# The first pair of rows of the first cross attention, made inside the last two heads of the first self attention

## The reference

```python
x = x + _L0_attn_ref(_layernorm(x), Wq, Wk, Wv, Wo, quadrant_weights)   # 16 heads of 16, 1024 x 1024 scores each
x = x + _L0_xattn_ref(_layernorm(x), ctx, ctx, ..., mask)               # below
x = x + _L0_ffn_ref(_layernorm(x), ...)                                 # top 2 of 8 experts, capacity 320
x = x + _L1_attn_ref(...); x = x + _L1_xattn_ref(...); x = x + _L1_ffn_ref(...)

def _L0_attn_ref(...):
    attn = softmax((q1 @ k_eff1.T + q2 @ k_eff2.T) * scale)
    return (attn @ v) @ Wo

def _L0_xattn_ref(q, k, v, ...):        # q: normalised x, k = v: the context
    qh, kh, vh = heads(q @ Wq.T + bq), heads(k @ Wk.T + bk), heads(v @ Wv.T + bv)
    scores = where(mask, qh @ kh.T / sqrt(16), -1000)
    return (softmax(scores) @ vh) @ Wo.T + bo
```

## Time and profile before

| | us |
|---|---|
| median of 3 runs | 1724.78 (1718.09 to 1725.84) |
| the profiled execution | 1716.94 |
| its span, first to last instruction | 1715.1 |
| mean granted TensorE clock, share of full speed | 0.969 |
| plain scores of the self attention (L2210), first to last start | 65.4 to 444.4 |
| turned scores of the self attention (L2219), first to last start | 84.4 to 465.2 |

### The profile page before, as it was taken

The page is one execution under the profiler, slowest core; times in us unless marked ns, Lnnn a source line. Parts: engine busy times, 40 slices in busy tenths (PEclk is TensorE's granted clock), DMA queues, the critical chain, the costliest instruction groups (busy, mean ns, idle before and its releaser), DMA issues. The chain is left out here.

```text
span 1715.1 us, 31331 instructions
## 1 busy us (share of the span) xinstructions
PE 1563.5 (91%) x10661; PEld 1106.5 (65%) x10662; DVE 973.9 (57%) x1748; ACT 585.2 (34%) x1167; POOL 404.9 (24%) x544
## 2 busy tenths in 40 slices
PE   6999999999889825999999999999989949999996
PEld 5733434343367624777777777856657649999995
DVE  7688888888369876221111211378879863444443
ACT  3277777777635500111111111034346500000000
POOL 1000000000022202233312211156652103333331
PEclk9999999999999966999999999999999969999998
DMA  2112221111401111133322331200015126666674
GB/s 75 39 46 66 58 55 47 42 45 43 166 21 36 45 51 32 22 99 104 102 64 52 95 89 16 55 11 1 2 59 175 50 90 175 176 179 181 181 183 117
DMA packets 89077, 134.90 MB, mean 79 GB/s; under 512 B 17568, under 2 KB 66080, under 8 KB 88832
## 3 DMA queue, kind: packets, MB, share of 16 engines
q1 hardware_dynamic: 73824, 113.05, 20.9%
q0 software_dynamic: 15168, 20.72, 7.6%
HBM read 98.00 MB, written 20.84 MB: 69 GB/s over the span
## 5 line engine op out<-in xcount | busy, mean ns | idle before, releaser
L2117 DVE TENSOR_REDUCE mx<-ps 128x1 f32<-128x1024 f32 x256 | 300.2, 1215 | 59.1 <-PE ps L2210 59.1
L1286 PE MATMUL ps<-xTe,wide 128*128 128x320 f32 x1024 | 277.2, 432 | 0.1
L1286 PEld LDWEIGHTS ps<-xTe,wide 128*128 128x128 f32 x1024 | 194.4, 190 | 80.2 <-issue 0.3
L1355 DVE TENSOR_TENSOR hTe<-prT,ps 128x320 f32<-128x320 f32 x128 | 62.4, 488 | 214.3 <-ACT prT L1327 214.1
L2016 ACT ACTIVATE wide<-ps 128x512 f32<-128x512 f32 x256 | 138.9, 599 | 61.0 <-PE ps L2219 61.0
L2016 ACT ACTIVATE turns_of_use<-ps 128x512 f32<-128x512 f32 x256 | 139.2, 600 | 59.1 <-PE ps L2219 58.8
L2219 PE MATMUL ps<-QS,KS 99*128 99x512 bf16 x512 | 154.2, 381 | 2.0 <-ACT wide L2016 0.8
L1445 PEld LDWEIGHTS ps<-xw_all,w1t 128*128 128x128 f32 x1248 | 145.3, 192 | 3.6 <-issue 0.9
L1445 PE MATMUL ps<-xw_all,w1t 128*128 128x128 f32 x1248 | 145.8, 275 | 1.2 <-ACT xw_all L1477 1.2
L1327 ACT ACTIVATE prT<-ps 128x320 f32<-128x320 f32 x128 | 55.9, 437 | 262.3 <-PE ps L1286 262.3
L1462 PE MATMUL ps<-wide,hTm 128*128 x624 | 141.0, 379 | 0.0
(11 more groups left out here) (305 smaller groups left out, 2328.9 us busy)
## 6 DMA issues: line engine op xcount, KB each, us to landing
w1t<-in_L_ffn_w SPq DMA_DIRECT2D x39, 1024.0 KB
wide<-in_L_ffn_gate_weight SPq DMA_DIRECT2D x8, 1024.0 KB, 5.5
wide<-_L_ffn_ff_pre_act_weight SPq DMA_DIRECT2D x8, 1024.0 KB, 8.6
wide<-L_ffn_ff_post_act_weight SPq DMA_DIRECT2D x8, 1024.0 KB, 10.9
wide<-in_L_ffn_w SPq DMA_DIRECT2D x1, 8192.0 KB, 27.2
QS<-wide SPq DMA_DIRECT2D x192, 32.0 KB, 2.0
KS<-wide SPq DMA_DIRECT2D x192, 32.0 KB, 2.0
VS<-V_all SPq DMA_DIRECT2D x32, 128.0 KB, 2.1
```

The source lines that it names most:

```text
L1286: ins = pe.matmul(ps[:, 3 + 2 * (q % 2) + n, 0:HC], wt[:, k, f * P:f * P + P], xTe[:, k, hf * HC:hf * HC + HC], start=(k == 0), stop=(k == ...
L1355: v.tensor_tensor(hTe[:, f, hf * HC:hf * HC + HC], sgt[:, q % 2, :], ps[:, 4 + 2 * (q % 2), 0:HC], ALU.mult).then_inc(f_m.sem, 1)
L2117: v.tensor_reduce(mx[:, s, t:t + 1], ps[:, 2 * (t % 2):2 * (t % 2) + 2, :], AX.XY, ALU.max).then_inc(h_rm.sem, 1)
```

## The change

Three parts.

1. Pair 0's rows, context, set-up, queries and first scores move from behind meeting 1 into heads 30 and 31. PE gets six blocks, each between two pieces of its attention work: turn pair 0's rows, the context, and the projection in head 30; turn the normalised rows, the queries and the scores in head 31. They use banks 0 (`FORE`) and 1 (`FORE_OWN`) in place of 7 and 6, and 2 and 3 as before. DVE gets `dve_first_rows` at the end of its part of head 30 and `dve_first_queries` at the end of its part of head 31, and does there what ACT did for this pair: the copies to `oT1` and `xT`, the normalised rows and the queries with their bias. POOL finishes pair 0's factors and adds the bias of pair 0 ahead of meeting 1.
2. The cross attention begins with pair 1's rows and pair 0's softmax. `keep_going(pe, 18, 1)` is gone. On DVE, pair 1's addition and statistics now stand between the two halves of pair 0's softmax; they stood before both.
3. `V_all` and `QS` are allocated first among the attention's tiles, so that the cross attention's tiles that are written early lie over `V_all`, whose last part has been read by then (`dve_first_rows` waits for the loads `h_ld` of all four slots).

```diff
+        V_all = sbA("V_all", [P, B, H, TB, 32])
+        QS = sbA("QS", [P, 4, S], BF16)
         turns_of_use = sbA("turns_of_use", [P, 4096])
...
+        def pe_first_rows(pe):
+            pe.wait_ge(x_ld, X_LOADS[0])
+            pe.wait_ge(h_rm.sem, h_rm.upto(B * H - 1))
+            pe_turn(pe, O_all[:, 0:2, :], x_ta, FORE)
+        def pe_first_projection(pe):
+            pe.wait_ge(x_oa.sem, x_oa.upto(0))
+            pe_out_rows(pe, oT1, woA, FORE_OWN, x_wa)
+        def pe_first_turn(pe):
+            pe.wait_ge(x_xn.sem, x_xn.upto(0))
+            pe_turn(pe, xn[:, 0, :, :], x_tb, FORE)
+        def pe_first_scores(pe):
+            pe.wait_ge(x_cr.sem, x_cr.upto(0))
+            pe.wait_ge(x_ra.sem, x_ra.upto(0))
+            pe_scores(pe, 0, 0, 0)
+        def dve_first_rows(v, c):
+            for sl in range(4):
+                v.wait_ge(h_ld[sl].sem, h_ld[sl].upto(B * H // 4 - 1))
+            v.wait_ge(x_ta.sem, x_ta.upto(0))
+            v.tensor_copy(oT1[:], by_chunk(FORE)).then_inc(x_oa.sem, 1)
+            dve_set_up(v, c, 0)
+            v.wait_ge(x_wa.sem, x_wa.upto(0))
+            v.tensor_tensor(pair_rows(0), pair_rows(0), ps[:, FORE_OWN, :].rearrange("p (j d) -> p j d", j=2), ALU.add)\
+                .then_inc(x_ra.sem, 1)
+            v.wait_ge(x_ra.sem, x_ra.upto(0))
+            c(row_stats(v, 0, 2))
+            begin_factors(v, 0, 2, x_fia)
+        def dve_first_queries(v):
+            v.wait_ge(x_fa.sem, x_fa.upto(0))
+            for t in range(2):
+                ins = v.tensor_scalar(xn[:, 0, t, :], xr[:, t, :], nv[:, 0, t:t + 1], nmr[:, t:t + 1], ALU.mult, ALU.add)
+            ins.then_inc(x_xn.sem, 1)
+            v.wait_ge(x_tb.sem, x_tb.upto(0))
+            v.tensor_copy(xT[:, 0, :, :], by_chunk(FORE)).then_inc(x_xt.sem, 1)
+            v.wait_ge(x_q.sem, x_q.upto(0))
+            for m in range(KC):
+                ins = v.tensor_scalar(qT[:, m, :], ps[:, FORE, m * 256:m * 256 + 256], float(DH) ** -0.5,
+                                      bq4[:, m:m + 1], ALU.mult, ALU.add)
+            ins.then_inc(x_qe.sem, 1)
...
             for i in range(-2, NP + 3):          # DVE
...
                 if here(i):
                     softmax(i, U, 0)
+                if layer == 0 and i == 0:
+                    v.wait_ge(x_wa.sem, x_wa.upto(1))
+                    add_rows(1, OWN, x_ra, 1)
+                    factors(1, x_fia)
...
-                if layer == 0 and here(i + 2):
+                if layer == 0 and 1 < i + 2 < NP:
...
-                if layer == 0 and i == -1:
-                    keep_going(pe, 18, 1)
...
             ahead_scores(t) of PE's head, called with t = 0, 2, 4, 6:
+                    elif (hh, t) == (2, 0):
+                        pe_first_rows(pe)
+                    elif (hh, t) == (2, 2):
+                        pe_context(pe, 0)
+                    elif (hh, t) == (2, 4):
+                        pe_first_projection(pe)
+                    elif (hh, t) == (3, 2):
+                        pe_first_turn(pe)
+                    elif (hh, t) == (3, 4):
+                        pe_queries(pe, 0, FORE)
+                    elif (hh, t) == (3, 6):
+                        pe_first_scores(pe)
```

More of the change, by code:

```diff
@@ L634, in act_cross @@
                     probs_turned(of(layer, i), 0)
-                if layer == 0 and here(i + 1):
+                if layer == 0 and 0 < i + 1 < NP:
                     queries(of(layer, i + 1))
@@ L785, in pool_cross, with pe_turn @@
                     end_factors(pool, c, i - 1, x_fid, x_fd, of(layer, i - 1))
-                if layer == 0 and here(i + 2):
-                    add_bias(i + 2, i + 2)
-        def pe_turn(pe, rows, done):
+                if layer == 0 and 0 < i + 2 < NP:
+                    pool_bias(pool, i + 2, i + 2)
+        def pe_turn(pe, rows, done, bank=TURN):
             for k in range(KC):
                 for j in range(2):
-                    ins = pe.transpose(ps[:, TURN, (2 * k + j) * P:(2 * k + j + 1) * P],
+                    ins = pe.transpose(ps[:, bank, (2 * k + j) * P:(2 * k + j + 1) * P],
@@ L794, in pe_turn, with pe_out_rows, pe_queries @@
                                        rows[:, j, k * P:(k + 1) * P], ident[:])
             ins.then_inc(done.sem, 1)
+        def pe_out_rows(pe, oT_, wo, bank, done):
+            for j in range(2):
+                for k in range(KC):
+                    ins = pe.matmul(ps[:, bank, j * 256:j * 256 + 256], oT_[:, k, j * P:j * P + P], wo[:, k, :],
+                                    start=(k == 0), stop=(k == KC - 1))
+            ins.then_inc(done.sem, 1)
+        def pe_queries(pe, U, bank):
+            pe.wait_ge(x_xt.sem, x_xt.upto(U))
+            for m in range(KC):
+                for k in range(KC):
+                    ins = pe.matmul(ps[:, bank, m * 256:m * 256 + 256], xw["q"][:, k, m * P:m * P + P],
+                                    xT[:, 0, k, :], start=(k == 0), stop=(k == KC - 1))
+            ins.then_inc(x_q.sem, 1)
@@ new lines, in pe_scores @@
+        def pe_scores(pe, u, U, j):
+            pe.wait_ge(x_qe.sem, x_qe.upto(U))
+            pe.wait_ge(x_sm.sem, x_sm.upto(U, j))
+            for m in range(KC):
+                for r in range(2):
+                    rows = slice(64 * r, 64 * r + 64)
+                    ins = pe.matmul(ps[:, r, m * 256:m * 256 + 256], qT[rows, m, j * P:j * P + P],
+                                    Kbd[rows, u // 4, m, :, :].rearrange("p h k -> p (h k)"),
+                                    start=True, stop=True)
+            ins.then_inc(x_s.sem, 1)
@@ L823, in pe_cross @@
         def pe_cross(pe, layer, left=None):
[L824 to L835, removed]
             def turn_prev(u):
@@ L843, in project_prev @@
                 pe.wait_ge(x_ra.sem, x_ra.upto(u - 1))
-                out_rows(oT1, woA, OWN, x_wa)
+                pe_out_rows(pe, oT1, woA, OWN, x_wa)
             def turn_out(u, U):
@@ L866, in logits @@
                 ins.then_inc(x_lg.sem, 1)
[L868 to L877, removed]
             def turn_probs(U, j):
@@ L908, in pe_cross @@
                 U = of(layer, i)
-                if i == -layer:
+                if layer == 1 and i == -1:
                     pe.wait_ge(x_cr.sem, x_cr.upto(layer))
-                if here(i):
-                    scores(i, U, 0)
+                if here(i) and (layer, i) != (0, 0):
+                    pe_scores(pe, i, U, 0)
                 if here(i - 1):
@@ L2144, in head @@
                     maxima(n + 2, hh % 2, 2, 8)
+                if last and hh == 2:
+                    dve_first_rows(v, c)
+                if last and hh == 3:
+                    dve_first_queries(v)
             maxima(0, 0, 0, 8)
```

55 lines of the change are left out of this document (25 added, 30 removed).

## The result

The changed kernel takes 1710.82 us (median of 6, 1708.83 to 1713.40) against 1724.42 (1718.09 to 1725.84): ratio 0.9933, 95% interval 0.9916 to 0.9951. It is faster by 13.6 us between the medians; by the ratio it is 0.7%, or 11.6 us (8.4 to 14.5). Forecast were 13.3 us and 1711.5.

A forecast was written before the change was run, and what follows sets the result against it. Around meeting 1 every engine waits for the next in a chain; in heads 30 and 31 PE and ACT take turns. The forecast was 1724.78 + 4.6 - 17.9 = 1711.5 us, range 1702 to 1719.5.

The forecast's parts named there:

- The meeting, +4.6: Heads 30 and 31: PE's 8.24 us of moved blocks, partly covered by waits, make meeting 1 4.6 us later.
- DVE under the blocks: Heads 30 and 31: DVE has 3.7 us to spare before head 30's division, so its new queue costs nothing.
- Behind the meeting, 12.8: From meeting 1 to pair 1's first scores: a chain of 12.8 us, before 30.69, so 17.9 us gone.
- No PE gap over 1.7 us: Behind meeting 1: the walk of the new order finds no PE gap longer than 1.7 us.
- a granted clock of 0.5 behind the meeting: Sign of being wrong: PE granted half clock behind meeting 1, where full clock was expected from 440 to 590.
- `keep_going` worth nothing: Kernel before, behind meeting 1: the 36 products, 4.18 us, ran during DVE's set-up and are worth nothing by themselves.
- The freely running watch: PE's clock: the same gap need not cost 1.7 us in another execution; gain then 11.6 instead of 13.3 us.
- Layout, later stages: The new allocation is priced at 0, up to 1 us either way; later stages start earlier and are the same.
- Sum: Whole kernel: +4.6 for the later meeting less 17.9 behind it gives -13.3 us.
- Uncovered blocks (9.2): Rival, 14%: in heads 30 and 31 PE's 8.24 us, with waits 9.2, come on top; gain 7.0 or 5.3 us.
- A longer chain through DVE (18): Rival, 8%: pair 1's scores no earlier than 18 us behind meeting 1; gain 8 us, time 1716.7.
- A clock that stays low: Rival, 4%: half clock at meeting 1 and the pairs behind; three pairs would give +26 us, 1751.

The follow-up runs named there:

- e4: The changed kernel with head 31's blocks (turn, queries, scores of pair 0, and their DVE and POOL work) put back behind meeting 1; trace span 1709.8 us.
- e5: The changed kernel with the context's 16 products made twice over in head 30; trace span 1713.5 us.
- e8: The changed kernel with five extra 128x1024 reductions on DVE in front of head 30's division; trace span 1716.2 us.
- e9: The changed kernel with products nobody reads filling PE's waits at the end of the first cross attention; ratio to the kernel before 0.9914.
- e3: The kernel before without the 18 `keep_going` products in turn -1; ratio to the kernel before 1.0014.
- e1: The kernel before with only the new layout, `V_all` and `QS` allocated first; ratio to the kernel before 1.0001.
- e11: The kernel before with products nobody reads filling the end of its first cross attention; ratio to the kernel before 0.9994.
- e0: The changed kernel once more, unedited; 1707.82 us against 1721.36 for the kernel before, ratio 0.9913.
- e6: The changed kernel with pair 1's addition and statistics on DVE behind both halves of pair 0's softmax; trace span 1716.0 us.
- e10: The changed kernel with products nobody reads at meeting 1 and at the end of the cross attention; ratio to the kernel before 0.9914.
- e12: The changed kernel with pair 1's addition behind both softmax halves and products nobody reads filling meeting 1; trace span 1718.0 us.

## Why the prediction was right

- **The meeting, +4.6.** Measured +5.0 (403.5, and 408.4 to 408.5 in two traces). Head 30: 3.0 forecast, 3.2 by e4; head 31: 1.6 forecast, 1.75. The misses are small: normalised rows 0.73 us on DVE, so PE's second turn waited 0.33 us. The step that each block's cover must be looked for piece by piece is confirmed by e5, where a block without cover costs its full length.
- **DVE under the blocks.** Right: 3.73 us to spare, and e8 shows that the wait begins where the spare time ends. I left out the clock there: "each us of lateness would cost PE one" is too low, it was 3.85 for 2.44 in the one trace of e8.
- **Behind the meeting, 12.8.** 12.4 to 12.7 at full clock, 13.8 and 13.9 in the two traces of the changed kernel. "No PE gap over 1.7 us" held: in these traces and in e9 the longest ahead of pair 1's scores is 1.35. The step that failed is the one from there to full clock. The meeting is a row of short waits (0.49, 0.68 and 0.72 us with little work between), and behind these together the projection halved as it did behind one gap of 3.40 us before, in five of six traces, and in none of the three with the waits filled. So one of my signs of being wrong, a granted clock of 0.5 behind the meeting, came true, at a price of 1.0 us.
- **`keep_going` worth nothing.** Wrong for the kernel before, by 1.4 us in the trace and 2.4 (0.3 to 4.3) in the times, e3. The wait of 4.4 us on PE cost clock for the next block. The changed kernel has no such wait, so the sum isn't touched.
- **The freely running watch.** The prediction took it from the Trainium skill (TensorE: Matmul & The Clock Gate, What's actually happening), which has the clock judged by a watch that does not start with the kernel. By that rule the gain was to be 11.6 where the 1.7 us of clock in the kernel before did not recur. They recurred in all four traces of the old order, at 1.6 us, and 2.7 in e1; e11 lost another 1.6 at the meeting. So b and c together are 11.9 to 14.7 us longer in these four traces than in the changed kernel's. That the same wait halves the clock in one execution and not in another is what d shows: 121.5 or 121.6 in three traces, 122.9 to 125.8 in eight, at the same 2.37 us.
- **Layout, later stages.** 0 by e1 (-1.7 to +2.1 us); d and e are the same work, with the clock of d as told above.
- **Sum.** -13.3 forecast, -11.9 in b and c of the first pair of traces: the blocks cost 0.4 us more and the clock behind the meeting 1.0. Between the medians it is -13.6, and -11.6 (-8.4 to -14.5) by the ratio; e0 has -13.5 and -15.0 (-12.6 to -17.4). That the first medians meet the sum within 0.3 us is in part luck, the size of some 12 to 15 us is not. The range's low end, 1702, has no working of its own: the sum beside it gives 1703.2.
- **Rivals.** Uncovered blocks (9.2): measured 5.0. A longer chain through DVE (18): 13.8, while e6 shows that it comes true when the addition stands behind the second half (19.1). A clock that stays low: it was low for one projection and came back.

## What to carry to other kernels

Work moved ahead of a barrier into another stage costs what that stage's bound engine can't hide; find it by walking that engine's waits one by one. After they are used up a microsecond costs a microsecond, as in e5. Work put between two halves of another engine's task can be worth more than the task it delays, if the next pair's chain starts from it. A walk that finds no long wait doesn't promise full clock: here three short waits in a row cost 1.0 us. And compare stretches between fixed points of two traces, not the spans: here differences in the other stretches hid 6.5 of 11.9 us.

## What the runs showed of the hardware

The first plain scores begin between 65.4 and 70.5 us (column a), for a reason 50 us earlier. In six traces they begin at 69.2 us or later, in the other eight at 67.1 or earlier. DVE's TENSOR_SCALAR on 128x256 float32 in SBUF takes 0.35 us where it has ended when POOL's sixteen memsets of `V_all` begin, and more where it is still under way then. First DVE and POOL in e0, then in e1:

```profile
11.73 0.35 DVE L2120 TENSOR_SCALAR turns_of_use<-turns_of_use,qsm 128x256 f32<-128x256 f32 x1
...
12.40 4.40 POOL L1999 MEMSET V_all<- 128x240 f32 x16
```

```profile
11.93 4.43 DVE L2074 TENSOR_SCALAR turns_of_use<-turns_of_use,qsm 128x256 f32<-128x256 f32 x1
16.39 0.48 DVE L2075 SCALAR_TENSOR_TENSOR turns_of_use<-turns_of_use,qsm 128x256 f32<-128x256 f32 x1
...
12.25 3.96 POOL L1954 MEMSET V_all<- 128x240 f32 x16
```

In 6 of the 14 traces, the six with the late first scores (e1, e5, e6, e8, e10, e12), this one instruction took 4.4 to 4.5 us, until the sixteenth memset had ended; in the others it took 0.34 to 0.96 us. Its start lies between 11.73 and 11.99 us. With the new layout it took long in all six traces where it began at 11.83 or later, and in none of the five where it began at 11.81 or earlier. In the three traces with the old layout it never did, though it began at 11.84 and 11.99 in two of them. So the layout may have a part in it. e1's ratio of 1.0001 (0.9990 to 1.0012) shows no cost on the mean, but its interval has room for up to 2 us. How much of the runs' spread of 8 us is due to it isn't shown: the kernel before spreads as far, and none of its traces has it. No run edited these memsets, so the cause is read from the coincidence. The Trainium skill (SBUF — State Buffer, SBUF: two separate sides) has VectorE, in its two-port modes, and GpSimd share one pair of ports under an exclusive lock, held for one instruction; the trace agrees that DVE stands still, but here it stood still over sixteen instructions in a row, in e5 and e6 though it had begun 0.04 us ahead of POOL's first memset. No run shows in which mode this instruction worked.
